# Layer norms of three batches made in the stage in front of two gates and one attention of a four-layer network

## The reference, cut to what matters

```python
h = tok(...)
h = h + L0_attn(_layernorm(h))     # causal linear attention, 16 heads
h = h + L0_ffn(_layernorm(h))      # 16 experts, top 2 of a softmax gate, norm at the end
h = h + L1_attn(_layernorm(h))
h = h + L1_ffn(_layernorm(h))      # graph attention gives the gate, 4 experts
h = h + L2_attn(_layernorm(h))     # key and value norms, no softmax
h = h + L2_ffn(_layernorm(h))      # 8 experts
h = h + L3_attn(_layernorm(h))
h = h + L3_ffn(_layernorm(h))
# L3_ffn: x = x + attention(rmsnorm(x, ln1)); flat = rmsnorm(x, ln2)
#         probs = softmax(flat @ router.T); top 2 of 8 experts; return x + out
```

## Time and profile before

| | us |
|---|---|
| median of 3 runs | 1054.52 (1050.43 to 1054.63) |
| the profiled execution | 1048.04 |
| its span, first to last instruction | 1046.0 |
| PE busy | 908.7 |
| DVE busy | 651.0 |
| ACT busy | 369.0 |
| POOL busy | 223.5 |

### The profile page before, as it was taken

How to read it: one execution, slowest core, us unless ns; L and a number is a source line. 1 busy time by engine, 2 the same in 40 slices (tenths; PEclk the granted TensorE clock), 3 DMA queues, 4 the chain that set the end, 5 groups by cost and what they waited for, 6 DMA issues and landing times. The chain is left out here.

```text
span 1046.0 us, 17260 instructions
## 1 busy us (share of the span) xinstructions
PE 908.7 (87%) x6702; PEld 452.8 (43%) x6702; DVE 651.0 (62%) x1734; ACT 369.0 (35%) x645; POOL 223.5 (21%) x291
## 2 busy tenths in 40 slices
PE   1888788879998864997888989999999889979998
PEld 0577566652323333762356333333333444443333
DVE  4977555676675273996565654555553655577665
ACT  0113532234542432232443514444445022453222
POOL 2600022215336020440140140121214412100000
PEclk9999898999999986996998988999999998999999
DMA  9300300000000001000000000000000000000000
GB/s 308 82 1 2 98 2 1 2 2 1 1 1 1 1 1 43 1 2 1 0 1 1 1 1 1 1 1 2 1 1 1 1 1 1 2 2 0 6 6 11
DMA packets 11478, 15.43 MB, mean 15 GB/s; under 512 B 8268, under 2 KB 9324, under 8 KB 10398
## 3 DMA queue, kind: packets, MB, share of 16 engines
q1 hardware_dynamic: 9976, 13.20, 4.1%
q10 hardware_dynamic: 1418, 1.09, 0.4%
HBM read 13.76 MB, written 0.52 MB: 14 GB/s over the span
## 5 line engine op out<-in xcount | busy, mean ns | idle before, releaser
L633 DVE TENSOR_REDUCE mx<-PS 128x2 f32<-128x1024 f32 (+3 forms) x104 | 109.7, 1096 | 97.9 <-PE PS L440 94.2
L593 ACT ACTIVATE arena<-PS 128x1024 f32<-128x1024 f32 (+3 forms) x104 | 91.1, 924 | 127.8 <-PE PS L470 127.8
L1231 DVE TENSOR_TENSOR arena<-arena,PS 128x512 f32<-128x512 f32 (+1 forms) x144 | 97.1, 685 | 49.2 <-ACT arena L1206 44.4
L1132 PE MATMUL PS<-XT,late 64*128 64x512 f32 (+1 forms) x288 | 103.1, 656 | 11.1 <-PEq L2516 6.6
L485 PE MATMUL PS<-arena 128*64 128x512 f32 (+3 forms) x416 | 100.1, 570 | 0.5 <-DVE arena L694 0.4
L1206 ACT ACTIVATE arena<-PS,f_b_sb 128x512 f32<-128x512 f32 x96 | 61.9, 686 | 67.3 <-PE PS L1132 65.9
L465 PE MATMUL PS<-arena 32*128 32x512 f32 (+4 forms) x416 | 76.8, 608 | 10.2 <-ACT arena L570 7.4
L1164 PE MATMUL PS<-arena,late 128*64 128x512 f32 (+1 forms) x288 | 82.8, 626 | 1.0 <-DVE arena L1231 0.9
L440 PE MATMUL PS<-arena 32*128 32x512 f32 (+4 forms) x416 | 69.1, 601 | 4.4 <-ACT arena L566 1.6
L1132 PEld LDWEIGHTS PS<-XT,late 64*128 64x128 f32 (+1 forms) x288 | 28.7, 186 | 63.7 <-ACT arena L1206 41.7
L1206 ACT ACTIVATE arena<-PS 114x512 f32<-114x512 f32 x48 | 27.4, 596 | 67.6 <-PE PS L1134 66.9
(11 more groups left out here) (427 smaller groups left out, 1650.6 us busy)
## 6 DMA issues: line engine op xcount, KB each, us to landing
arena<-in_rel SPq DMA_DIRECT2D x4, 1024.0 KB, 12.0
late<-in_edges SPq DMA_DIRECT2D x2, 1024.0 KB, 11.3
late<-in_w_f_w SPq DMA_DIRECT2D x3, 342.0 KB
arena<-in_adj SPq DMA_DIRECT2D x1, 1024.0 KB, 6.9
late<-in_w_f_w SPq DMA_DIRECT2D x2, 512.0 KB, 3.7
Cc<-in_consts SPq DMA_DIRECT2D x1, 916.0 KB
arena<-in_ids ACTq DMA_DIRECT2D x1, 800.0 KB
late<-in_w_f_w SPq DMA_DIRECT2D x4, 128.0 KB, 3.2
```

The lines of the kernel that those rows point to most:

```text
L593: nc.scalar.activation(PT[:, s % 2, p, :, queries(c)], PS[:, a:a + 2, queries(c)], ACT.Exp, scale=scale).then_inc(exp_done.sem, 1)
L633: v.reduce_max(mx[:, g % 2, c, 2 * p:2 * p + 2], PS[:, a:a + 2, keys(c)], axis=AX.X).then_inc(max_done.sem, 1)
L1132: ins = nc.tensor.matmul(PS[0:rows, up_bank(n), :], w1(i)[r], XT2[r, b * S:(b + 1) * S], start=True, stop=True)
L1231: nc.vector.tensor_tensor(HG[0:rows, n % 4, :], ha, PS[0:rows, gate_bank(n), :], ALU.mult).then_inc(gated_done.sem, 1)
```

## The change

- `Entering` objects are made for the norms ahead of layer 0's gate, layer 2's attention and the last gate, and passed to the stages in front and to `entry` as `ahead`.
- `linear_attention`: VectorE does `sums` of batch q at the end of groups 2, 4 and 6, after a wait for GpSimd's additions, and `root` behind the masks of groups 3, 5 and 7. GpSimd does `centre` and `apply` behind the additions of every second group.
- `softmax_attention` with `rope`: GpSimd does `centre` at c = 1 and `apply` at c = 3; VectorE's calls in it were there for other uses (`sums` has nothing to do without centring, but the wait ahead of it stands).
- layer 1's experts get `after`, as layer 0's and layer 2's have.
- `entry` with `ahead`: GpSimd does `centre` and `apply` of quarter 3 ahead of `aside`, VectorE `sums` and `root`; no norms of its own, no Sqrt table. TensorE does two filler products, turns and projects quarters 0 to 2, then waits for four steps of quarter 3's norm with two filler products behind each, then turns and projects quarter 3.
- the last experts wait for the residual sum of the last batch (`complete`).

```diff
@@ -764,8 +764,13 @@
                         outs(g - 1)
                         for q in done_with(g - 1) if after is not None else ():
                             for i in range(len(after.norms)):
+                                if i == 0:
+                                    eng.wait_ge(heads_added.sem, at(heads_added, 2 * g * NPAIR - 1))
                                 after.centre(eng, q, i)
-                                after.apply(eng, q, i)
+                                if not rope:
+                                    after.apply(eng, q, i)
+                    if after is not None and rope and c == 3 and g >= 1:
+                        after.apply(eng, g - 1, 0)
                 eng.wait_ge(heads_added.sem, at(heads_added, 2 * (G - 1) * NPAIR - 1))
...
@@ -787,7 +792,7 @@
...
-    def linear_attention(G, batch, project, vo_src, vo_of, values, dst, eps):
+    def linear_attention(G, batch, project, vo_src, vo_of, values, dst, eps, after):
...
+
+        after.opened()
+        normed_at = {2 * q + 3: q for q in range(B - 1)}
...
+                    if g in normed_at:
+                        after.root(eng, normed_at[g], 0)
                     if g >= 1:
                         outs(g - 1)
                     draw(eng, g)
                     if g + 2 < G:
                         elu(g + 2)
+                    if g + 1 in normed_at:
+                        eng.wait_ge(heads_added.sem, at(heads_added, 4 * g - 1))
+                        after.sums(eng, normed_at[g + 1], 0)
                 outs(G - 1)
 
             @block.gpsimd
@@ -1027,6 +1040,9 @@
                             eng.wait_ge(heads_added.sem, at(heads_added, 2 * n + j - 1))
                         y = dst[:, b * TB:(b + 1) * TB, :]
                         nc.gpsimd.tensor_tensor(y, y, ON[:, n % 2, j, :].rearrange("p (c d) -> p c d", d=D), ALU.add).then_inc(heads_added.sem, 1)
+                    if n % 4 == 3:
+                        after.centre(eng, n // 4, 0)
+                        after.apply(eng, n // 4, 0)
...
@@ -1237,6 +1253,8 @@
...
+                        if ahead is not None and b == B - 1:
+                            ahead.complete(eng, b)
                         nc.vector.tensor_tensor(dst[:, y, :], PS[:, out_bank(b), 0:TB * D].rearrange("p (t d) -> p t d", d=D), base[:, y, :], ALU.add).then_inc(out_added.sem, 1)
...
+        def complete(self, eng, q):
+            eng.wait_ge(norm_steps[q].sem, self.base[q] + self.steps)
...
         with (nc.Block() if block is None else nullcontext(block)) as block:
+            if ahead is not None:
+                @block.gpsimd
+                def _(eng):
+                    ahead.centre(eng, last, 0)
+                    ahead.apply(eng, last, 0)
+
             if aside is not None:
                 @block.gpsimd
...
                     v.tensor_scalar(w_, w_, by, None, ALU.mult).then_inc(weights_scaled.sem, 1)
+                if ahead is not None:
+                    ahead.sums(eng, last, 0)
+                    ahead.root(eng, last, 0)
...
-                    eng.wait_ge(norm_steps[q].sem, nv[q] + ready)
+                    if ahead is None:
+                        eng.wait_ge(norm_steps[q].sem, nv[q] + ready)
+                    else:
+                        ahead.normed(eng, q)
...
-                def dense(n):
+                def dense(n, a=6):
...
-                        nc.tensor.matmul(PS[:, 6, :], identh[:], bc(identh[:], 1, TB), start=True, stop=True, skip_group_check=True)
...
+                        nc.tensor.matmul(PS[:, a, :], identh[:], bc(identh[:], 1, TB), start=True, stop=True, skip_group_check=True)
+
+                if ahead is not None:
+                    dense(2)
...
                 for q in range(5):
+                    if ahead is not None and q == last:
+                        if proj:
+                            project(q - 1)
+                        for k in range(ahead.ready - 4, ahead.ready):
+                            eng.wait_ge(norm_steps[q].sem, ahead.base[q] + k)
+                            dense(2, q)
                     if turned is not None and q < 4:
                         turn(q)
-                    if proj and q >= 1:
+                    if proj and q >= 1 and (ahead is None or q != last):
                         project(q - 1)
...
-        linear_attention(2 * B, lambda g, j: g // 2, project, MV[:], lambda g, p: 2 * (g % 2) + p, X, H, 1e-9)
+        linear_attention(2 * B, lambda g, j: g // 2, project, MV[:], lambda g, p: 2 * (g % 2) + p, X, H, 1e-9, after)
...
-    def l2_attn():
-        entry([Norm(H, X)], turned=XT2[:], aside=kv_weights)
+    def l2_attn(ahead):
+        entry(ahead=ahead, turned=XT2[:], aside=kv_weights)
...
-            entry([Norm(X, R, eps=1e-6, center=False, gamma=row("f3_ln2"), plus=(Y, H, X))], turned=XT2[:],
+            entry(ahead=after, turned=XT2[:],
...
-    l0_attn()
+    to_gates = Entering([Norm(H, X)])
+    l0_attn(to_gates)
...
+    to_mixing = Entering([Norm(H, X)])
+    l1_ffn(to_mixing)
+    l2_attn(to_mixing)
...
+    to_gates = Entering([Norm(X, R, eps=1e-6, center=False, gamma=row("f3_ln2"), plus=(Y, H, X))])
+    l3_ffn(to_causal, to_gates)
```

More of the change, by code:

```diff
@@ L1079, in _program, with experts @@
     out_added = Signal(ctx, nc, "out_added")
-    def experts(E, T, rows, w1, w2, act_fn, gate, base, dst, b1=None, w3=None, b2=None, store=False, aside=None, block=None, entered=None, between=None, after=None):
+    def experts(E, T, rows, w1, w2, act_fn, gate, base, dst, b1=None, w3=None, b2=None, store=False, aside=None, block=None, entered=None, between=None, after=None, ahead=None):
         tiles = [(b, i) for b in range(B) for i in range(T)]
@@ L1802, in turned_out, with entry @@
             nc.scalar.copy(XT2[:, q * S:(q + 1) * S], PS[:, a, :]).then_inc(turned_copied.sem, 1)
-    def entry(norms=(), turned=None, proj=(), gates=None, products=None, scales=(), late=False, aside=None, block=None, then=None, beside=None):
+    def entry(norms=(), turned=None, proj=(), gates=None, products=None, scales=(), late=False, aside=None, block=None, then=None, beside=None, ahead=None):
         quarter = lambda q: slice(q * TB, (q + 1) * TB)
+        last = B - 1
+        if ahead is not None:
+            ahead.received()
         first = [sum(m.steps for m in norms[:i]) for i in range(len(norms))]
```

25 lines of the change are left out of this document (12 added, 13 removed).

## The result

| kernel | median us (range, runs) | ratio to before, same chip [95%] | profiled execution, us | its span | mean granted clock |
|---|---|---|---|---|---|
| before | 1052.47 (1047.59 to 1054.63, 4) | | 1048.04 | 1046.0 | 0.945 |
| changed | 1073.27 (1064.51 to 1080.51, 4) | 1.0173 [1.0097, 1.0249] | 1080.51 | 1078.7 | 0.908 |
| changed, second set of runs | 1072.66 (1064.25 to 1075.08, 6) | 1.0196 [1.0151, 1.0240] | 1072.76 | 1070.9 | 0.918 |

The forecast was 1057.5, the range 1052.5 to 1063.0; the kernel landed above all of it, and even rival 1, more low clock, was put at 1063.5. A ratio leaves out the executions that are over 1.5% above the fastest of their kernel, while a median holds them all. The profile of the first set is of its longest execution, so the second profile (span 1070.9) is read beside it.

The account below looks back on a forecast made before the run. A loop through three engines was taken to pace the first attention; elsewhere stages were read block by block. Terms -0.3 - 1.6 + 4.8 = +2.9 us gave 1050.9 us profiled, 1057.5 us for the median; range 1052.5 to 1063.

Parts of the forecast that it names:

- rival 1: More low clock: one more slow loop turn (+3.1) and 7 us behind GpSimd's queue (+3); +9, 1063.5 us; chance 0.25.
- 2 x 0.6 = +1.2: First attention's loop: VectorE's reduction and scaling ahead of the mask cost 0.6 us in two groups, +1.2 us.
- rival 3: 16-way entry: 7 us of low clock bring project 3 at 233.5, no gain there; +2 on the sum, 1059.5; chance 0.12.
- rival 4: Causal attention: contention hits every collision, 3.4 us in place of 0.4; +3, 1060.5; chance 0.06.
- windows at 0.50 where there were none: Sign in the new profile that the forecast is wrong and rival 1, more low clock, holds.
- The 16-way gate: Entry with that gate: VectorE starts the second half at 231.5 in place of 232.97, -1.5 us.
- The chain of one batch: Each entry: one batch's norm through GpSimd takes 4.5 us from its first reduction.
- The last gate: Its entry: VectorE starts the second half at 934.05 in place of 936.09, -2.0 us.
- +0.4: Layer 3's causal attention: GpSimd's last steps meet VectorE's zeroing of later keys, 0.57 a collision, +0.4 us in all.
- +2.0: Layer 1's experts: third batch's addition to the next block takes 5.83 us in place of 3.78, +2.0 us.
- +2.3: Layer 2's attention entry: last batch's GpSimd steps queue ahead of 18 weight steps, +1.9 to +2.5, taken as +2.3 us.
- +0.5 with 0 and +3 as ends: Layer 2's attention: ScalarE's exposed Sqrt table load and low clock after TensorE's idle, +0.5 us together.

Follow-up runs that it names:

- delay_only_c: Kernel before plus only a VectorE reduction and scaling, results unused, between elu and mask in groups 2, 4 and 6 of linear attention; 1065.13 us, ratio 1.0115.
- gate16_filled_d: Layer 0's part of the change alone, in its own order, plus four unread TensorE products in groups 3 and 5; 1053.93 us, ratio 0.9994 to before.
- sums_moved_c: Layer 0's part of the change alone, with VectorE's sums moved behind the mask and the root one step later; 1056.45 us, ratio 0.9998 to before.
- lastgate_only: Changed kernel with only the norms ahead of the last gate, the other entries put back; 1049.28 us, ratio 1.0006 to before.
- before_filled: Kernel before plus two unread TensorE products in every group of the linear attention; 1047.72 us, ratio 0.9983.
- layer2_only: Changed kernel with only the norms ahead of layer 2's two-head attention, the other entries put back; 1057.35 us, ratio 1.0091 to before.
- two_gates_filled: Both gates' parts without layer 2's, sums behind the mask, two unread products in every group of linear attention; 1046.10 us, ratio 0.9954 to before.
- gate16_only: Changed kernel with only the norms ahead of the first 16-way gate, the other entries put back; 1070.99 us, ratio 1.0174 to before.
- layer2_vector_d: Layer 2's part of the change alone, with the 18 weight steps on VectorE in place of GpSimd; 1053.73 us, ratio 0.9991 to before.
- all_mended: All three parts of the change, with sums behind the mask and layer 2's weight steps on VectorE; 1054.50 us, ratio 0.9994 to before.
- all_mended_filled: all_mended plus two unread TensorE products in every group of the linear attention; 1045.28 us, ratio 0.9942 to before.

## Why the prediction was wrong, step by step

**The loop of the linear attention: the arithmetic was right, the consequence missed.** "2 x 0.6 = +1.2" was 2 x 0.52. (The forecast counts turns from zero: its turns 2 and 4 are the third and the fifth here.) The step that failed stands in rival 1: "six turns with the same pauses ran at full clock" was taken as evidence against more low clock. But they were pauses of the old length, and one of the seven turns was slow even so the earlier trace rows; so full clock was not assured even at that length. A longer pause in two turns made three turns slow: +8.7 us for a delay of 1.0, shown by delay_only_c, and undone by filling the pause in gate16_filled_d or by moving the sums behind the mask in sums_moved_c. Behind it the layer-0 experts lost another 3.6 us in a stretch at the lower level. Together that is 12.3 of the 24.9 us by which the second profile is longer.

The Trainium skill, "TensorE: Matmul & The Clock Gate", section "A second HAM failure mode: psum-queue depth-cycling", tells of a kernel that cycles through PSUM banks and whose short idles between groups of matmuls, frequent enough, made the clock switch back and forth. The trace agrees that short idles can be enough: no pause for the mask is over 1.11 us, and the stage's clock went from 0.94 to 0.86. But here the pauses grew longer and not more frequent.

**Rival 1's price was short.** It gave "one more such turn +3.1" and "+3" behind the GpSimd queue. Measured: two slow turns more and one worse, a low stretch in the experts, and in layer 2 an attention longer by 5.6 us. The rival was priced once per place; the trace has it over whole stages. Its chances slipped a little as well: rival 1 with a third of (3) and (4) is 0.25 + 0.06 = 0.31, not 0.29. The prediction's own sign for it, "windows at 0.50 where there were none", was there to be read: 10 us in the layer-0 experts, none before. The range needed this case at its full size, some 1,070 us.

**The 16-way gate: order right, size wrong, and rival 3 near the truth.** Eight fillers run right ahead of the last turn, and VectorE idles 1.85 us between the halves ("about 2" was forecast). TensorE in the entry of the changed kernel, its clock over the first 5 us, and VectorE's two halves:

```profile
236.23 1.01 PE L2085 MATMUL PS<-identh 128*128 128x512 bf16 x2 [2.93 <-PEq L838]
237.17 3.68 PE L2072 MATMUL PS<-Cc,X 128*64 128x128 f32 x32
...
244.00 1.90 PE L2085 MATMUL PS<-identh 128*128 128x512 bf16 x8
245.83 1.09 PE L2072 MATMUL PS<-Cc,X 128*64 128x128 f32 x16
```

```profile
236.23:241.20 4.97, 4.97 (x38) 0.50 0.00 0
```

```profile
243.36 0.29 DVE L1905 TENSOR_TENSOR L<-PS,f_gate_b_sb 128x128 f32<-128x128 f32 x1 [4.46 <-PE PS L2080]
...
248.28 0.29 DVE L1905 TENSOR_TENSOR L<-PS,f_gate_b_sb 128x128 f32<-128x128 f32 x1 [1.85 <-PE PS L2080]
```

The second half starts 12.05 us after the block's first instruction; before it was 12.32 (232.97 - 220.65). The forecast had 10.85. The step that failed is the clock at the block's start. The sum put the two first fillers at full speed (0.5 us), the two turns at "1.97 us of work, of which 1.4 at half speed" (3.35) and the first projection at full speed (0.55), 4.4 us in all. Nearly all of it ran at the lower level and took 5.4, since the low stretch lasted 5.0 us here, not the 2.7 of the earlier trace rows. The norms ahead put needed work where only filler had run. So the second half gains 0.3 us in this profile, and the stage nothing (19.7 us both times). Over all profiles the stage took 18.4 to 19.7 us with the part and 19.7 to 20.6 without. The chain of one batch was right: 4.45 us (236.23 to 240.68, the end of GpSimd's multiply) for 4.5.

**The last gate: right.** The second half was to come at 9.65 us from the block's start and came at 968.74 - 959.18 = 9.56; before it was 11.68. The stage fell from 18.59 to 16.48, and every profile has it so: 16.5 with the part, 18.6 without.

```profile
968.74 0.23 DVE L1903 COPY L<-PS 128x64 f32<-128x64 f32 x1 [2.10 <-PE PS L2080]
```

**The causal attention in front of it: rival 4 falls, but +0.4 was too little.** TensorE's products that waited for the zeroing of later keys (us, times), first before, then in the changed kernel's second profile:

```profile
  PE PS L485: 0.4, 1
```

```profile
  PE PS L485: 0.7, 2
```

That is 0.3 us more of TensorE, so the zeroing costs nothing like the rival's 3.4. But the block itself, with the same 10 us at the lower level, went from 107.7 to 108.5 us: +0.8. Some 0.7 of it is at its end, which the forecast put at nothing. VectorE's last additions, with both inputs in SBUF like the zeroing, now run beside GpSimd's gain and residual sum. VectorE before, then VectorE and GpSimd in the changed kernel:

```profile
921.38 0.89 DVE L674 TENSOR_TENSOR X<-X,arena 128x256 f32<-128x256 f32 x2
```

```profile
955.45 1.58 DVE L674 TENSOR_TENSOR X<-X,arena 128x256 f32<-128x256 f32 x2
```

```profile
955.15 0.73 POOL L1799 TENSOR_TENSOR R<-R,f_ln_sb 128x256 f32<-128x256 f32 x1
955.96 0.79 POOL L1803 TENSOR_TENSOR Y<-H,X 128x256 f32<-128x256 f32 x1
```

The second profile has the same 1.58 us, and TensorE then idles 1.64 us ahead of the next block in place of 0.94.

**Layer 2, the tail and the entry: right in mechanism.** From the third batch's addition to the next block was to be 5.83 us and is 540.87 - 535.05 = 5.82. The stretch of the experts grew by 2.5 us for a forecast of +2.0; at equal time at the lower level it is 2.0 (31.0 us in lastgate_only and 33.0 here with 10 us low, 27.1 in before_filled and 29.1 in layer2_only with 2). VectorE there:

```profile
535.05 0.42 DVE L1258 TENSOR_TENSOR H<-PS,H 128x256 f32<-128x256 f32 x1
...
540.87 0.42 DVE L1763 TENSOR_REDUCE st<-H 128x4 f32<-128x256 f32 x1 [1.81 <-PEq L2765]
```

GpSimd runs the norm's last multiply and then the 18 weight steps, and its last copy ends the block:

```profile
544.71 0.61 POOL L1794 TENSOR_TENSOR X<-tA,st 128x256 f32<-128x256 f32 x1
545.26 0.53 POOL L2806 COPY arena<-late 128x64 f32<-128x64 f32 x2
...
551.04 0.24 POOL L2815 COPY arena<-a_vln_b_sb 128x64 f32<-128x64 f32 x1
551.78 2.35 POOL L2913 TENSOR_TENSOR H<-H,X 128x1024 f32<-128x1024 f32 x1 [0.50 <-SPq L2824]
```

The weight steps took 6.0 us (545.26 to 551.28), a little under the 6.2 that the lower end supposed, and the entry 10.92: +1.8 for a forecast of +2.3.

**Layer 2's attention: the term "+0.5 with 0 and +3 as ends" was mis-sized.** The stage is 5.6 us longer, though not all of that is the part's, as said below. Two things are in the rows. Eight products over the queries take 7.08 us at the lower level, after TensorE had idled 3.03 us while GpSimd ended. And ScalarE's table load stands before the first root. TensorE, then ScalarE:

```profile
551.79 1.81 PE L2831 MATMUL PS<-arena,XT 64*128 64x128 f32 x16 [3.03 <-PEq L1847]
553.53 7.08 PE L2864 MATMUL PS<-XT,late 64*64 64x512 f32 x8
```

```profile
554.15 1.28 ACT L2897 ACT_TABLE_LOAD   x1
555.45 0.31 ACT L2897 ACTIVATE chan<-chan 128x128 f32<-128x128 f32 x1
```

Eight such products took 3.64 us in the kernel before. Of the load's 1.28 us about 0.6 is exposed: the root starts 1.32 us behind the activation ahead of the load, and in the kernel before, without a load there, it started 0.75 us behind it, waiting for VectorE.

The Trainium skill, "ScalarE: Activation LUTs", section "What ACT_TABLE_LOAD costs", adds a drain of about 1.38 us to each load. Here the next activation starts 0.02 us after the load's end, so the row supports leaving that drain out.

**What stays open.** The layer-2 attention takes 33.3 us in before, sums_moved_c, before_filled and two_gates_filled, and 36.0 to 36.4 in gate16_only, lastgate_only, delay_only_c and gate16_filled_d, which leave layer 2 as it was. It takes 36.0 to 36.5 in layer2_only, layer2_vector_d, all_mended and all_mended_filled, too; 38.9 came only with the whole change. In code that is the same, the layer-2 gate goes between 18.4 and 20.4, the last stretch of layer 1's experts between 27.1 and 31.0, the opening between 105.7 and 114.0, and the layer-3 attentions between 313.9 and 318.2, with more or less time at the lower level. No run here tells what picks one of them.

So of the 24.9 us, 12.3 (the linear attention and the experts behind it), 4.4 (tail and entry of layer 2, some 0.5 of it low clock) and -2.1 (last gate) are placed at the part that makes them. The 3.6 of the experts in it are placed only at the part as a whole with its delay. The opening's 2.4 us are in code that the change doesn't touch. Of the 7.6 us in the layer-2 attention and gate, about 4.6 also come in kernels without that part; the rest is argued to be the load and the longer low stretch, not shown.

## What to carry to other kernels

Before work is put into a loop of several engines, look at the clock in that loop's turns: if one in seven already runs at the lower level, as here, give a rival that prices half a microsecond of added pause at whole slow turns a real chance. Put the work behind the instruction that the other engines wait for, or give TensorE unread products for the pause; either took this loop's loss away. And what is taken out of an entry is worth only what its next-latest engine leaves: here work at the low clock, a shared GpSimd queue and eight fillers ahead of the last turn kept most of it.

## What the runs showed of the hardware

TensorE's clock in this loop reacts to half-microsecond differences of one pause. With the pause at 0.59 us, five of six profiles have one slow turn (14.8 us) behind the first turn, and the sixth, of an execution near the top of its kernel's range, has two. At 1.11 us in two turns, all four profiles have three slow turns. With those two filled, or with all of them filled (1.3 us in seven turns in place of 4.4), none of four profiles has one. A turn that was itself longer, 12.21 us, ran at a clock of 1.00 once its pause was filled, and in gate16_only with the pause at its full length.

TensorE idled 3.0 to 3.1 us ahead of the layer-2 attention in three profiles, and stood at the lower level within 0.5 us of the block's start in each. With an idle of 0.94 us, in the eleven others, the first eight products over the queries ran in 3.6 us, at the upper level.

The same code runs a whole stage at lengths that fall into two groups: the layer-2 attention 33.3 or 36.0 to 36.4 us, the layer-2 gate 18.4 to 18.7 or 19.9 to 20.4. That is wider than most effects that one wants to measure, so a stage has to be compared over several kernels before a difference is put down to an edit.

VectorE's additions of 128x256 with both inputs in SBUF took 1.58 us a pair beside GpSimd's elementwise work in all six profiles with the last gate's part, and 0.9 without it.
